# Attention heads in groups of four on TensorE, and a null product over all 128 rows

## The chip, the cores and the metric

The kernel runs on one core of one Trainium2 chip. The metric is device time in microseconds (us) of one execution. The times before are three runs; the profile is one further execution, whose own time and span are given below.

## What is computed

Eight batches of 256 rows and 128 features go through an attention layer with 16 heads of 64, then through a gated feed-forward network (FFN) with quantised weights and activations, and the result is added to the input. In short:

```
xn = ln(x) * g_norm
q = xn @ Wq (16 heads of 64);  k, v = halves of xn @ Wkv   (one k and v for all heads)
k, v = [null_kv ; k], [null_kv ; v]                        (one null key ahead of the 256)
sim = 8 * (q/|q| * q_scale) @ (k/|k| * k_scale).T + bias   (null bias, relative position bias from an MLP)
attn = softmax(causal(sim));  out = attn @ v
y = ln(out @ Wout) * g_out
x + FFN(y)      (y and the hidden layer quantised to 8 bits by their largest magnitude)
```

The causal mask is known ahead: rows 0 to 127 need 129 keys, rows 128 to 255 need 257.

## The kernel before

Five engines run programs of their own and meet at semaphores. After a prologue (bias table, projections of batch 0) comes the main part, a sequence of steps, one for each head of each batch: 16 steps for batch 0 ("first"), 96 for batches 1 to 6, 16 for batch 7 ("last") and 16 more to drain ("flush"). `over_batches` calls `step` on every engine; the order of the work is written out by hand, as lags in steps behind the scores of a head.

For a pair of heads, TensorE makes the scores with a contraction over 64 rows (L758): the two heads of a pair sit on the upper and lower 64 rows and their products run side by side, into `score_ps[0]` and `score_ps[1]`. That pair of PSUM banks is the only one, so the scores of the next pair wait for semaphore `scored`. VectorE adds the bias and finds the row maxima (L1084). ScalarE takes exponents with the row sums (L574), VectorE inverts the sums (L1090), GpSimd multiplies (L434). Five steps behind, TensorE transposes the probabilities in three 128x128 pieces (L769), ScalarE copies them to `pT` (L543), and eight steps behind TensorE multiplies them with v (L850): there the output has 64 columns for a head, and the two heads again run side by side into the two halves of `val_ps`. VectorE copies that to `oT` (L1076), TensorE multiplies by Wout (L736) into `misc`, summing over all heads of the batch. A float32 product is issued as two passes, so L758 and L850 have eight passes for a pair of heads.

The null key's share of the output is a product of its own: `null_weights` transposes the null probabilities of 16 heads (L729), ScalarE copies them to `pnT`, 16 rows, and L826 multiplies by `unull`, 16 rows, and closes the sum in `misc`.

In the same steps the next batch is prepared: x is normalised (L920) and transposed (L616), kv (L622), k (L629); q is made in four quarters (L636), squared (L487), its norm summed (L948), raised to the power -1/2 on GpSimd (L388), normalised (L954), transposed (L652) and copied to `qT` (L959). The previous batch's y gets its statistics (L1112), is normalised (L1119), transposed (L833), scaled (L1147). One PSUM bank, `qT_ps`, serves all these transposes in turn.

In the drained steps the FFN's weights are quantised on VectorE (`ffn_weights`) and turned on TensorE. Then `amax` (L1181) starts the FFN.

So on TensorE an even step is scores (64 rows), transposes and other work of full rows and columns, and an odd step is transposes, then values (64 columns).

Of the kernel before, what the change touches and what calls it, by code (L numbers as in the profile page):

```python
# [54 lines left out]
L_EXP, L_RECIP, L_NORM, L_TRANS, L_EVAC, L_VAL, L_OUT = 1, 2, 2, 5, 6, 8, 9  # L55

Q_FIRST = 4
Q_SQUARE, Q_POWER, Q_NORMALISE, Q_TRANS, Q_SPLIT = 1, 2, 3, 4, 5

FLUSH = 16  # L60


class Step:


    def __init__(self, b, parity, h, kind="loop"):
        self.b, self.parity, self.h, self.kind = b, parity, h, kind
        self.live = kind != "flush"

        self.next = (b + 1, 1 - parity) if kind in ("loop", "first") else None  # L70
        self.prev = (b - 1, 1 - parity) if kind != "first" else None

    def head(self, lag):

        h = self.h - lag
        if h >= 0:
            return (self.b * H + h, self.parity, h) if self.live else None
        return ((self.b - 1) * H + h + H, 1 - self.parity, h + H) if self.kind != "first" else None

    def quarter(self, lag):  # L80


        h = self.h - lag - Q_FIRST
        if h % 4 or not (self.next if h >= 0 else self.kind in ("loop", "last")):
            return None
        n, parity = self.next if h >= 0 else (self.b, self.parity)
        q = h % H // 4
        return 4 * n + q, q, parity

    def pair(self, lag):  # L90

        h = self.h - lag
        return self.b * HP + h // 2 if h >= 0 else (self.b - 1) * HP + (h + H) // 2
# [9 lines left out]
def over_batches(eng, step):  # L103

    for h in range(H):
        step(Step(0, 0, h, "first"))
    for b in range(1, B - 1):
        for h in range(H):
            step(Step(b, b % 2, h))
    for h in range(H):  # L110
        step(Step(B - 1, 1, h, "last"))
    for h in range(FLUSH):
        step(Step(B, 0, h, "flush"))


def build(nc, x, cond, mask, g_norm, Wq, Wkv, q_scale, k_scale, null_bias, w0, b0, g0, w1, b1, g1, w2, b2,
# [3 lines left out]
    with ExitStack() as ctx:  # L120
# [32 lines left out]
        unull = sb("unull", [H, C])  # L153
# [55 lines left out]
        pnT = sb("pnT", [H, N])  # L209
# [61 lines left out]
        null_column = sem("null_column")  # L271
# [98 lines left out]
        def _(pool):  # L370
# [44 lines left out]
            pool.memset(vnull[:, :, :], 0.0).then_inc(consts, 1)  # L415
            mlp_power(1)
# [7 lines left out]
            def step(s):  # L424
                if s.next and s.h == 8:
                    k_power(s.next[0])
                if quarter := s.quarter(Q_POWER):
                    c, q, _ = quarter
                    q_power(c, q)
                if head := s.head(L_NORM):  # L430
                    g, par, h = head
                    held(pool, inverted, g + 1, pool_passed)
# [3 lines left out]
                if s.kind == "last" and s.h == 10:  # L436
# [3 lines left out]
                if s.next and s.h == 0:  # L440
                    x_power(s.next[0])
                if s.prev and s.h == 12:
                    y_power(s.prev[0])

            over_batches(pool, step)
# [12 lines left out]
        def _(act):  # L458
# [13 lines left out]
            def v_copy(n, par):  # L472

                if not isinstance(n, int) or n > 1:
                    act.wait_ge(o_done, HP * (n - 1))
# [8 lines left out]
            def q_square(c, ps):  # L484
                act.wait_ge(q_done, c + 1)
                act.wait_ge(q_n2, c) if not isinstance(c, int) or c > 0 else None
# [37 lines left out]
            def ffn_weights(h):  # L524

                if h in (11, 12, 13):
                    k = h - 11
                    act.wait_ge(w_t, k + 1)
                    act.copy(wT[:, k, :, :], score_ps[k % 2][:, 0:IT * P].rearrange("p (t c) -> p t c", t=IT))\
                       .then_inc(w_a, 1)  # L530
                if h == 14:
# [3 lines left out]
            def step(s):  # L535
                if head := s.head(L_EVAC):
                    g, par, h = head
                    act.wait_ge(pT_done, g + 1)

                    pair = s.pair(L_EVAC)  # L540
                    if not isinstance(pair, int) or pair > 1:
                        act.wait_ge(o_done, pair - 1)
                    act.copy(pT[:, h % 4, :], trans_ps[h % 2][:, 0:3 * P]).then_inc(pT_ready, 1)  # L543
                if s.next:
                    n, par = s.next
                    if s.h == 3:
                        xT_evac(n, par, qT_ps)
                    if s.h == 7:
                        kv_evac(n, qT_ps)
                    if s.h == 11:  # L550
                        kT_evac(n, par, qT_ps)
                    if s.h == 10:
                        v_copy(n, par)
                if quarter := s.quarter(Q_SQUARE):
                    q_square(quarter[0], q_ps)
                if s.kind == "first":
                    if s.h == 11:
                        act.wait_ge(unull_done, 1)
                        act.copy(unull[:, :], misc[0:H, 0:C]).then_inc(unull_ready, 1)
                    if s.h == 15:  # L560
                        act.wait_ge(ld_misc, 16 * 5)
                        act.activation(sig[:, :], clips[:, :], ACT.Exp, scale=-1.0).then_inc(sig_exp, 1)
                if s.kind == "flush":
                    ffn_weights(s.h)
                if s.prev and s.h == 7:
                    m, _ = s.prev
                    act.wait_ge(n_done, m + 1)
                    act.copy(pnT[:, :], null_out).then_inc(n_ready, 1)
                if head := s.head(L_EXP):
                    g, par, h = head  # L570
                    for t, cols in ((1, slice(0, KEYS1)), (0, slice(KEYS1, KEYS1 + KEYS0))):

                        act.wait_ge(scored, 2 * g + (1 if t else 2))
                        act.activation(prob[:, par, h, cols], score[:, h % 4, cols], ACT.Exp, scale=-1.0,  # L574
                                       bias=negmax[:, par, h, t:t + 1],
                                       accum_out=rowsum[:, par, h, t:t + 1]).then_inc(exped, 1)

            over_batches(act, step)
# [33 lines left out]
        def _(pe):  # L612
# [33 lines left out]
            def qT_make(c):  # L646
                pe.wait_ge(q_norm, c + 1)
                if not isinstance(c, int) or c > 0:
                    pe.wait_ge(qT_ready, c)
# [614 lines left out]
```

## Time and profile before

| | us |
|---|---|
| median of three runs (lowest, highest) | 321.32 (320.86, 322.37) |
| the profiled execution | 322.74 |
| its span, first to last instruction | 320.9 |
| TensorE busy in the span | 275.6 |
| VectorE, ScalarE, GpSimd busy | 251.8, 228.5, 209.9 |
| mean granted TensorE clock | 0.961 |
| one step each on the way: subtraction for `wql` (L1102), two heads normalised on GpSimd (L434, four instructions) | 1.20, 1.66 |

Busy time counts an instruction from its start to its end. On TensorE a pass starts before the one ahead of it has ended, so the distance between starts says what a pass costs, and its duration does not. The same holds to a lesser degree on VectorE and ScalarE.

### The profile page before, as it was taken

The page shows a single profiled execution, that of the slowest core. Times are in us where ns is not written, and L with a number is a line of the kernel's source. Part 1 is how long each engine was busy: PE and PEld are TensorE (multiplying, and loading weights), DVE is VectorE, ACT ScalarE, POOL GpSimd, SP SyncE. Part 2 cuts the span into 40 slices and gives each one's busy share as a digit, 9 for nine tenths or more (in the row PEclk, how much of TensorE's full clock was granted, in tenths as well). Part 3 has the DMA queues.
Part 4 walks back from the last instruction along what each step waited for, and adds up shares of the span by engine and source line. Part 5 has one row for each costly group of instructions (what it writes and reads, how often), then busy time and mean ns, then how long its engine had stood idle before and what let it go on. Part 6 is the DMA issues. An engine that isn't in the chain of part 4 may idle for free.

```text
span 320.9 us, 7447 instructions
## 1 busy us (share of the span) xinstructions
PE 275.6 (86%) x2151; PEld 205.2 (64%) x2152; DVE 251.8 (78%) x1068; ACT 228.5 (71%) x771; POOL 209.9 (65%) x395
## 2 busy tenths in 40 slices
PE   0797899999899989998999899989998998956341
PEld 0345677787678767876777678767876776731031
DVE  3877887877887788778877887788778766848995
ACT  1454688887788778877887788778877897436761
POOL 3665797786778677767776778678867746311413
PEclk9999799999999999999999999999999999975957
DMA  4459000000000000000000000000000002000004
GB/s 140 109 129 224 1 1 3 0 2 1 3 0 3 3 1 2 0 3 1 3 0 3 0 3 3 0 0 4 3 0 2 1 3 67 2 2 0 0 2 135
DMA packets 13084, 6.90 MB, mean 21 GB/s; under 512 B 1953, under 2 KB 12913, under 8 KB 13042
## 3 DMA queue, kind: packets, MB, share of 16 engines
q1 hardware_dynamic: 12466, 6.13, 7.2%
q8 instruction: 20, 0.33, 0.4%
q10 hardware_dynamic: 576, 0.26, 0.3%
q14 instruction: 22, 0.18, 0.2%
HBM read 5.31 MB, written 1.07 MB: 20 GB/s over the span
## 4 chain that ended last, share of the span: by engine, by line
PE 56%; DVE 24%; POOL 10%; issue 5%; DMA 1%; ACT 1%; ACTq 0%; POOLq 0%; DVEq 0%
PE bank L758 12%; PE bank L850 12%; PE bank L769 10%; PE bank L736 7%; PE bank L636 4%; DVE score L1084 3%; PE bank L652 3%; POOL rq L388 3%; POOL prob L434 3%; DVE qT L959 2%; DVE qn L948 2%; DVE hmax L1171 2%; DVE oT L1213 2%; POOL ors L388 2%; DVE xn L920 2%
## 5 line engine op out<-in xcount | busy, mean ns | idle before, releaser
L434 POOL TENSOR_SCALAR prob<-prob,rrow 128x258 f32<-128x258 f32 (+1 forms) x256 | 109.9, 446 | 50.1 <-DVE rrow L1090 47.0
L574 ACT ACTIVATE prob<-score,negmax 128x258 f32<-128x258 f32 (+1 forms) x256 | 114.4, 451 | 10.5 <-DVE negmax L1084 10.5
L1084 DVE CUSTOM_DVE_ANT_0 score<-bank,bias 128x258 f32<-128x258 f32 (+1 forms) x256 | 80.5, 352 | 22.5 <-PE bank L758 21.7
L543 ACT COPY pT<-bank 128x384 f32<-128x384 f32 x128 | 61.1, 478 | 31.2 <-PE bank L850 29.1
L769 PE MATMUL bank<-ident,prob 128*128 128x128 f32 x384 | 66.7, 283 | 0.0
L758 PE MATMUL bank<-kT,qT 64*128 64x258 f32 (+1 forms) x512 | 60.1, 354 | 1.2 <-DVE negmax L1084 1.0
L388 POOL TENSOR_TENSOR rq<-qn,neghalf 128x8 f32<-128x8 f32 x32 | 54.2, 1694 | 2.7
L850 PE MATMUL bank<-pT,val 128*64 128x256 f32 (+1 forms) x512 | 55.7, 338 | 0.1
L758 PEld LDWEIGHTS bank<-kT,qT 64*128 64x128 f32 x512 | 44.7, 188 | 15.6 <-issue 11.0
L574 ACT ACTIVATION_READ_ACCUMULATOR prob<-score,negmax 128x1 f32 x256 | 48.8, 191 | 0.0
L769 PEld LDWEIGHTS bank<-ident,prob 128*128 128x128 f32 x384 | 42.5, 141 | 8.9 <-issue 0.3
L850 PEld LDWEIGHTS bank<-pT,val 128*64 128x64 f32 x512 | 31.2, 136 | 20.0 <-issue 9.9
L736 PE MATMUL bank<-wout,oT 128*128 128x128 f32 x256 | 37.9, 276 | 0.0
L1076 DVE COPY oT<-bank 128x256 f32<-128x256 f32 x64 | 26.7, 418 | 11.7 <-PE bank L850 10.3
L736 PEld LDWEIGHTS bank<-wout,oT 128*128 128x128 f32 x256 | 33.0, 192 | 0.2 <-issue 0.2
L948 DVE TENSOR_REDUCE qn<-sq 128x8 f32<-128x512 f32 x32 | 21.7, 679 | 6.5 <-ACT sq L487 6.5
L487 ACT ACTIVATE sq<-bank 128x512 f32<-128x512 f32 x32 | 19.1, 598 | 9.9 <-PE bank L636 6.2
L954 DVE TENSOR_TENSOR qn<-bank,rq 128x512 f32<-128x512 f32 x32 | 21.7, 679 | 0.6 <-POOL rq L388 0.4
L959 DVE COPY qT<-bank 128x512 f32<-128x512 f32 x32 | 21.7, 679 | 0.2 <-PE bank L652 0.2
L1084 DVE DVE_READ_ACCUMULATOR2_ANT negmax<- 128x1 f32 x256 | 21.0, 82 | 0.0
L652 PE MATMUL bank<-ident,qn 128*128 128x128 f32 x128 | 20.0, 281 | 0.9 <-DVE qn L954 0.9
L1090 DVE RECIPROCAL rrow<-rowsum 128x2 f32<-128x2 f32 x128 | 20.4, 160 | 0.2 <-ACT prob L574 0.2
(157 smaller groups left out, 344.4 us busy)
## 6 DMA issues: line engine op xcount, KB each, us to landing
bias<-relative_table SPq DMA_DIRECT2D x8, 256.0 KB, 5.2
out_dram<-prob SPq DMA_DIRECT2D x4, 256.0 KB, 2.6
X<-in_x_dram SPq DMA_DIRECT2D x1, 896.0 KB, 12.2
prob<-in_L_cond_Wq_dram SPq DMA_DIRECT2D x1, 512.0 KB, 5.8
wout<-in_L_cond_Wout_dram SPq DMA_DIRECT2D x1, 512.0 KB, 13.4
prob<-in_L_ffn_w_down_dram SPq DMA_DIRECT2D x1, 176.0 KB, 2.5
X<-in_x_dram SPq DMA_DIRECT2D x1, 128.0 KB, 4.2
prob<-in_L_ffn_w_gate_dram SPq DMA_DIRECT2D x1, 128.0 KB, 2.1
```

The costliest lines, as they stand in the source:

```text
L388: pool.tensor_tensor(dst, src, neghalf[:, 0:width], ALU.pow).then_inc(done, 1)
L434: pool.tensor_scalar(prob[:, par, h, cols], prob[:, par, h, cols], rrow[:, par, h, t:t + 1], 1.0, ALU.mult, ALU.mult).then_inc(normed, 1)
L543: act.copy(pT[:, h % 4, :], trans_ps[h % 2][:, 0:3 * P]).then_inc(pT_ready, 1)
L574: act.activation(prob[:, par, h, cols], score[:, h % 4, cols], ACT.Exp, scale=-1.0, bias=negmax[:, par, h, t:t + 1], accum_out=rowsum[:, p ...
L652: last = pe.transpose(qT_ps[:, k * P:k * P + P], head_pair, ident[:, :])
L736: pe.matmul(y_out(t), oT[:, par, k, t * P:t * P + P], wout[:, k, :], start=k + t == 0, stop=False, skip_group_check=True)
L758: product = pe.matmul(score_ps[a][:, at:at + KEYS1 - c0], qT[s.parity][rows, k, t * P:t * P + P], kT[s.parity][rows, c0:KEYS1], start=not ...
L769: last = pe.transpose(trans_ps[h % 2][:, k * P:k * P + P], prob[:, par, h, c0:c0 + P], ident[:, :])
L850: last = pe.matmul(val_ps[a * D:a * D + D, i0:N], val[par][:, blk, :], pT[:, (h - 1 + a) % 4, c0:c1], start=blk == 1, stop=blk == 0, skip_ ...
L948: dve.tensor_reduce(qn2[:, q, :], sq[:, :, :], AX.X, ALU.add).then_inc(q_n2, 1)
L959: dve.tensor_copy(qT[par][:, 4 * (q // 2):4 * (q // 2) + 4, P * (q % 2):P * (q % 2) + P], qT_ps[:, :].rearrange("p (k i) -> p k i", k=4)). ...
L1084: dve.tensor_tensor_reduce(score[:, slot, c0:c0 + w], ps[:, c0:c0 + w], bias[:, s.h, 0:w], -1.0, -3.0 * NEG, ALU.add, ALU.min, negmax[:, p ...
```

## The change

Steps of one head become groups of four. There are 34 groups, four for each of eight batches and two to drain; `Group` has the group's number `at`, the batch `b` and the place `g` (0 to 3) in it.

TensorE's order in a group is now: scores of its first pair of heads (A); values of all four heads of the group before the last one, into a whole PSUM bank; scores of its second pair (B); then everything with full rows: transposes of two heads of the last group, qT of a quarter, the next quarter's q, transposes of the other two heads, y products, and the transposes and products of x, kv, k, y. Before the last of these a wait for the qT copy of the quarter (`qT_ready`) stands in each group.

VectorE copies values to `oT` once for four heads (512 columns) and inverts row sums once for a pair (128x4). The null product's operands `pnT` and `unull` get 128 rows, of which 112 are zero, set by two memsets on GpSimd. Filler transposes behind the first scores are 10 instead of 16. In the last group the turns of the FFN's weights stand ahead of the last y products; the last batch's y is finished after the groups.

```
+        pnT = sb("pnT", [P, N])            # was [H, N]; unull likewise
+            pool.memset(unull[:, :], 0.0).then_inc(null_zero, 1)
+            pool.memset(pnT[:, :], 0.0).then_inc(null_zero, 1)
...
+            def values(at):
+                m, g = at // GB, at % GB
+                pe.wait_ge(pT_ready, GH * (at + 1))
+                if g == 0:
+                    pe.wait_ge(v_ready, m + 1)
+                if at > 0:
+                    pe.wait_ge(oT_ready, at)
+                for pair in range(2):
+                    for blk, c0, c1, i0 in ((1, 0, N, 0), (0, N, N + P, P)):
+                        for a in range(2):
+                            last = pe.matmul(val_ps[a * D:a * D + D, pair * N + i0:pair * N + N], val[m % 2][:, blk, :],
+                                             pT[:, 2 * pair + a, c0:c1], start=blk == 1, stop=blk == 0,
+                                             skip_group_check=True)
+                last.then_inc(o_done, 1)
...
+            def group(s, masked):                                   # TensorE
+                turned = s.at - 1 if 1 <= s.at <= GB * B else None
+                summed = s.at - 2 if s.at >= 2 else None
+                if s.live:
...
+                    scores(s, 0, masked)
+                if summed is not None:
+                    values(summed)
+                if s.at == 0:
+                    keep_busy(10)
+                if s.live:
+                    scores(s, 1, masked)
+                if turned is not None:
+                    turn(turned, 0)
+                    turn(turned, 1)
+                if s.quarter is not None:
...
+                    qT_make(s.quarter)
+                if s.made is not None:
...
+                    q_make(s.made, s.made % 4, s.made // 4 % 2, q_ps)
+                if turned is not None:
+                    turn(turned, 2)
+                    turn(turned, 3)
+                if s.at == GB * B + 1:
+                    for k in range(3):
+                        w_turn(k)
+                    down_scale_turn()
+                if summed is not None:
+                    y_products(summed)
+                if s.g == 1 and s.prev is not None:
+                    y_null(s.prev)
+                if s.quarter is not None:
+                    pe.wait_ge(qT_ready, s.quarter + 1)
+                if s.g == 0 and s.prev is not None:
...
+                    null_weights(s.prev)
+                if s.next is not None:
+                    if s.g == 0:
+                        xT_make(s.next, qT_ps)
+                    if s.g == 1:
+                        kv_make(s.next, qT_ps)
+                    if s.g == 2:
+                        kT_make(s.next, qT_ps)
+                if s.first and s.g == 1:
+                    null_output()
+                if s.g == 3 and s.prev is not None:
+                    yT_make(s.prev)
...
+            def group(s):                                           # VectorE
...
+                if s.live:
+                    score_pair(heads(s.at)[0:2])
+                if s.g == 0 and s.b > 1:
+                    yT_evac(s.b - 2)
+                if s.g == 2 and s.prev is not None:
+                    y_stats(s.prev)
+                if s.g == 2 and s.next is not None:
+                    k_norm2(s.next)
+                if s.g == 1 and s.next is not None:
+                    xT_split_low(s.next, s.next % 2)
+                if s.g == 0 and s.next is not None and not s.first:
+                    x_normalise(s.next)
+                if s.quarter is not None:
+                    q_normalise(s.quarter, s.quarter % 4, q_ps0[s.quarter] if s.quarter < 4 else q_ps)
+                if s.at >= 2:
+                    oT_copy(s.at - 2)
...
+                if s.live:
+                    score_pair(heads(s.at)[2:4])
+                    invert(heads(s.at)[0:2])
+                if s.g == 2 and s.prev is not None:
+                    y_normalise(s.prev)
+                if s.g == 2 and s.next is not None:
+                    k_normalise(s.next)
...
+                if s.quarter is not None:
+                    qT_evac(s.quarter, s.quarter % 4, s.quarter // 4 % 2)
+                if s.g == 3 and s.b + 2 < B:
+                    x_stats(s.b + 2)
+                if s.made is not None:
+                    q_norm2(s.made, s.made % 4)
+                if s.live:
+                    invert(heads(s.at)[2:4])
```

ScalarE's order in a group: exponents of heads 0 and 1, pT copies of the last group's heads 0 and 1, exponents of head 2, the square of a quarter of q, pT copy 2, exponents of head 3, pT copy 3, then the copies for x, kv, v, k. GpSimd's: the power for a quarter of q, normalisation of the last group's second pair, the powers for y and k (g = 2), normalisation of this group's first pair, the power for x (g = 3).

## Rows read from the trace of the kernel before

**Rows 1.** The page, part 1: busy time, share of the span and instructions

```profile
PE 275.6 (86%) x2151; PEld 205.2 (64%) x2152; DVE 251.8 (78%) x1068; ACT 228.5 (71%) x771; POOL 209.9 (65%) x395
```

**Rows 2.** Windows by batch: stretch, its length, busy time by engine, granted clock

```profile
26.38:55.44 29.06, 26.45 (x202) 20.49 (x202) 23.33 (x109) 20.66 (x80) 21.27 (x38) 0.94 0.17 40
55.44:87.23 31.79, 30.37 (x255) 23.67 (x253) 25.33 (x120) 25.26 (x90) 23.78 (x46) 1.00 0.01 2
...
214.38:246.17 31.79, 30.37 (x254) 23.68 (x253) 25.93 (x122) 25.27 (x90) 23.96 (x47) 1.00 0.01 2
246.17:287.84 41.67, 37.55 (x319) 28.72 (x317) 28.81 (x132) 29.10 (x99) 19.87 (x47) 0.97 0.06 15
```

**Rows 3.** Timeline of TensorE around one pair of heads: start, us, merged instructions

```profile
150.00 0.87 PE L850 MATMUL bank<-pT,val 128*64 128x256 f32 x8
150.80 0.93 PE L758 MATMUL bank<-kT,qT 64*128 64x258 f32 x8
151.66 0.55 PE L769 MATMUL bank<-ident,prob 128*128 128x128 f32 x3
...
152.75 0.60 PE L652 MATMUL bank<-ident,qn 128*128 128x128 f32 x4
153.18 0.61 PE L736 MATMUL bank<-wout,oT 128*128 128x128 f32 x4
153.63 0.49 PE L769 MATMUL bank<-ident,prob 128*128 128x128 f32 x3
```

**Rows 4.** The same in narrow windows: later passes of the same two blocks

```profile
150.49 0.39 PE L850 MATMUL bank<-pT,val 128*64 128x128 f32 x4
...
151.34 0.39 PE L758 MATMUL bank<-kT,qT 64*128 64x129 f32 x4
```

**Rows 5.** Timeline of TensorE around the null product

```profile
140.00 0.61 PE L736 MATMUL bank<-wout,oT 128*128 128x128 f32 x4
140.54 0.71 PE L826 MATMUL bank<-unull,pnT 16*128 16x128 f32 x4
141.18 0.55 PE L769 MATMUL bank<-ident,prob 128*128 128x128 f32 x3
```

**Rows 6.** Timeline of TensorE: its two idle stretches in a batch, with the releaser

```profile
116.63 0.44 PE L833 MATMUL bank<-ident,yn 128*128 128x128 f32 x2 [0.96 <-DVE qT L959]
...
124.93 0.44 PE L616 MATMUL bank<-ident,xn 128*128 128x128 f32 x2 [0.46 <-DVE qT L959]
```

**Rows 7.** Timeline: the other engines' starts within a batch

```profile
130.92 0.93 PE L758 MATMUL bank<-kT,qT 64*128 64x258 f32 x8
...
132.03 0.43 DVE L1084 CUSTOM_DVE_ANT_0 score<-bank,bias 128x258 f32<-128x258 f32 x1 [0.57 <-PE bank L758]
...
132.67 0.41 DVE L1084 CUSTOM_DVE_ANT_0 score<-bank,bias 128x258 f32<-128x258 f32 x1
...
155.02 0.48 ACT L543 COPY pT<-bank 128x384 f32<-128x384 f32 x1 [0.60 <-PE bank L850]
155.40 0.67 DVE L948 TENSOR_REDUCE qn<-sq 128x8 f32<-128x512 f32 x1
155.40 0.51 ACT L574 ACTIVATE prob<-score,negmax 128x258 f32<-128x258 f32 x1
...
155.99 0.68 DVE L959 COPY qT<-bank 128x512 f32<-128x512 f32 x1
...
156.29 0.48 ACT L543 COPY pT<-bank 128x384 f32<-128x384 f32 x1
...
156.59 1.67 POOL L388 TENSOR_TENSOR rq<-qn,neghalf 128x8 f32<-128x8 f32 x1
```

**Rows 8.** Timeline of TensorE at the last null product

```profile
282.36 0.71 PE L826 MATMUL bank<-unull,pnT 16*128 16x128 f32 x4
```

**Rows 9.** Window of one block of scores in batch 0, columns as in rows 2

```profile
33.37:34.96 1.59, 1.59 (x9) 1.18 (x8) 1.42 (x2) 1.48 (x7) 1.43 (x1) 0.50 0.00 0
```

More of the change, by code:

```diff
@@ L52, with __init__, heads @@
 TABW = N + P - 1
[L55 to L93, printed above, removed]
+GB = 4
+GH = H // GB
+class Group:
+    def __init__(self, at):
+        self.at = at
+        self.b, self.g = at // GB, at % GB
+        self.par = self.b % 2
+        self.live = self.b < B
+        self.first = self.b == 0
+        self.next = self.b + 1 if self.b + 1 < B else None
+        self.prev = self.b - 1 if self.b > 0 else None
+        c = GB * self.b + self.g + 2
+        self.quarter = c if c < GB * B else None
+        self.made = c + 1 if 4 <= c + 1 < GB * B else None
+def heads(at):
+    b, h = at // GB, at % GB * GH
+    return [(b * H + h + i, b % 2, h + i) for i in range(GH)]
 def held(eng, sem, value, passed):
@@ L100, in held, with over_groups @@
     eng.sem_inc(passed, 1)
[L103 to L113, printed above, removed]
+def over_groups(group):
+    for at in range(GB * B + 2):
+        group(Group(at))
 def build(nc, x, cond, mask, g_norm, Wq, Wkv, q_scale, k_scale, null_bias, w0, b0, g0, w1, b1, g1, w2, b2,
@@ L422, in _, with normalise @@
                 q_power(q, q)
[L424 to L432, printed above, removed]
+            def normalise(pair):
+                held(pool, inverted, pair[0][0] // 2 + 1, pool_passed)
+                for _, par, h in pair:
                     for t, cols in ((1, slice(0, KEYS1)), (0, slice(KEYS1, KEYS1 + KEYS0))):
@@ L439, in step @@
                     pool.memset(wrow[:, 2, IT - 1, IL:P], 0.0).then_inc(w_pad, 1)
[L440 to L445, printed above, removed]
+            over_groups(group)
+            y_power(B - 1)
             for k in range(4):
@@ L522, in _, with exponent @@
             act.copy(wqh[:, :], wq[:, :]).then_inc(wq_high, 1)
[L524 to L531, printed above, removed]
+            def exponent(head):
+                g, par, h = head
+                for t, cols in ((1, slice(0, KEYS1)), (0, slice(KEYS1, KEYS1 + KEYS0))):
+                    act.wait_ge(scored, 2 * g + (1 if t else 2))
+                    act.activation(prob[:, par, h, cols], score[:, h % 4, cols], ACT.Exp, scale=-1.0,
+                                   bias=negmax[:, par, h, t:t + 1],
+                                   accum_out=rowsum[:, par, h, t:t + 1]).then_inc(exped, 1)
@@ L532, in ffn_weights @@
                     act.wait_ge(w_t, 4)
                     act.copy(sdrow[:, :], score_ps[1][:, 0:C]).then_inc(w_a, 1)
[L535 to L576, printed above, removed]
@@ new lines, in scores @@
+            def scores(s, pair, masked):
+                g, par, h = heads(s.at)[2 * pair]
+                if g > 0:
+                    pe.wait_ge(scored, 2 * g)
+                if masked:
+                    for a in range(2):
+                        pe.matmul(score_ps[a][:, 0:KEYS1 + KEYS0], ones_row[:, :], mrow[:, s.b, 0:KEYS1 + KEYS0],
+                                  start=True, stop=True)
+                for t, at, c0 in ((1, 0, 0), (0, KEYS1, P + 1)):
+                    for a in range(2):
+                        rows = slice(a * D, a * D + D)
+                        product = pe.matmul(score_ps[a][:, at:at + KEYS1 - c0],
+                                            qT[par][rows, h // 2, t * P:t * P + P], kT[par][rows, c0:KEYS1],
+                                            start=not masked, stop=True, skip_group_check=True)
+                        if t == 0:
+                            product.then_inc(s_done, 1)
@@ new lines, in group @@
+                if s.made is not None:
+                    if s.made % 4 == 0:
+                        if s.first:
+                            pe.wait_ge(wq_low, 1)
+                        pe.wait_ge(xT_low, s.next)
+                    q_make(s.made, s.made % 4, s.made // 4 % 2, q_ps)
+                if turned is not None:
+                    turn(turned, 2)
+                    turn(turned, 3)
+                if s.at == GB * B + 1:
+                    for k in range(3):
+                        w_turn(k)
+                    down_scale_turn()
@@ L1155, in scales @@
+            over_groups(group)
+            y_stats(B - 1)
+            y_normalise(B - 1)
+            yT_evac(B - 1)
             def scales(k):
```

413 lines of the change are left out of this document (188 added, 225 removed).

## Prediction, made before the changed kernel ran

> **What bounds the kernel now.** I read the page first: TensorE 86% busy, VectorE 78, ScalarE 71, GpSimd 65 [rows 1]. Four engines this full cannot be ranked by shares of a whole run, so next came the table by stage, cut at the first score product of each batch [rows 2]. Batches 1 to 6 take 31.79 us each, to the hundredth, with TensorE busy 30.4, VectorE 25.9, ScalarE 25.3 and GpSimd 24.0. TensorE hardly stops there, at a granted clock of 1.00, its 2.4 GHz level. Then I read the timeline of TensorE alone, since a busy TensorE need not be a working one [rows 3 to 6].
>
> Inside a block of one shape its passes start at even distances: four passes of 128 columns take 0.43 to 0.45, so 0.109 each, and a pass of 256 columns costs twice that, 0.216 [rows 3, 4]. Between shapes the distance grows. A block of values, eight passes in four side-by-side pairs, needs 2 x 0.216 + 2 x 0.109 = 0.65 and takes 0.80: 0.05 is lost before its third pair (0.49 from its start instead of 0.43), 0.10 before the next block. A block of scores takes 0.86 where 0.65 would do: 0.11 lost at its start (0.54 to its third pair), 0.10 at its end. The full-row block behind it loses 0.06 at its start (three transposes take 0.55, where those that follow a full-row product take 0.49) and 0.10 at its end (140.00 to 140.54 for four passes that need 0.44) [rows 3 to 5]. One pair of heads has three changes of shape and loses 0.15 + 0.21 + 0.16 = 0.52; eight pairs are 4.2 a batch. The null product on 16 rows adds two more: 0.64 for four passes that need 0.44, 0.10 lost ahead of it and 0.06 behind, 0.36 a batch [rows 5].
>
> The rest are real waits: the transposes of yn and of xn stand idle for 0.96 and 0.46 until VectorE has copied qT [rows 6]. With the weight loads that such a wait uncovers they make up the remainder. The books of a batch: 31.79 = 25.4 of streaming + 4.2 + 0.36 + 1.86 of waits.
>
> **The change, part by part.**
>
> *Shapes.* In four heads the order was scores, full rows, values, full rows and so on, six changes. Now it is scores A, values of two pairs, scores B, full rows: four changes, 2 x 0.21 + 0.15 + 0.16 = 0.73 instead of 1.04, so 0.31 x 4 = 1.26 saved a batch. Scores followed directly by values is a neighbourhood that the trace does not show. I take the 0.10 with which every block ends and the 0.05 with which values start, since in the three neighbourhoods seen each end costs the same. Bounds: nothing at all, 0.15 x 4 = 0.6 more saved; as dear as the entry of scores, 0.05 x 4 = 0.2 lost. The Trainium skill (TensorEngine Tiling (Array Packing), Key Properties) says that changing the tiling mode, not just the tile, drains TensorE; it gives no price, and the gaps above agree with it.
>
> *Null product over 128 rows.* The same four passes without a change of shape: 0.36 saved a batch, 2.9 in eight. It can't be less than 0: the y products ahead of it write the same tile at 0.11 a pass. The Trainium skill (TensorEngine Tiling (Array Packing), When to Use Tiling) advises four-fold row tiling for a contraction of up to 32, which speaks against this edit: by it the 16 rows would be the cheap form. The row shows no two of the four passes side by side, and the 0.64 against 0.44, so the measurement decides. The two memsets for it are on GpSimd before batch 0 and end before the first normalisation needs it.
>
> Without any wait a batch would take 25.4 + 2.9 + 0.3 (a small gap before scores B, below) = 28.6.
>
> *VectorE.* Eight oT copies of 256 columns become four of 512, 0.60 apart as L948 and L959 are; sixteen reciprocals become eight. Its 25.9 falls to about 24.5. ScalarE and GpSimd keep their work. The FFN weights' memsets and DMAs move to g = 1 of the last batch, some 15 us before VectorE reads them.
>
> *Waits, by walking one group on four engines.* Distances between starts: scores of a head on VectorE 0.56 (0.64 with an inversion), 512 columns 0.60, exponents of a head 0.89, pT copy 0.38 [rows 7], square 0.50, GpSimd 0.84 a head; a q power is 0.33 + 1.67 and begins 0.2 behind its input. VectorE starts on scores 1.11 after their block began (130.92, 132.03) [rows 7]. Time 0 is TensorE's start on scores A.
>
> g = 3, the plain group. VectorE works on A from 1.11 to 2.23. TensorE ends values at 2.31, but B may start only when both heads of A are released, 2.37: 0.06 lost in every group. B reaches VectorE at 3.48; until then it does q normalise and oT, to 3.44. TensorE: two turns to 3.94, qT 4.38, q 5.08, turns 5.73, y 6.60, yT, next group 6.93. ScalarE: exponents 1.62 to 3.42, two pT copies to 4.58, exponent 5.48, square, pT, exponent, pT to 7.65; values of the next group want that pT at 7.8. The last pair is inverted at 7.6, 0.44 before the next scores reach VectorE. GpSimd: the next group's q power ends 2.0 to 2.4 into it, where VectorE wants it at 2.24.
>
> g = 0: VectorE first evacuates yT (0.85) and normalises x (0.62), so qn is late and qT starts at 4.44, not 3.94: with null and x transposes 7.65. g = 1: y null and kv, four passes each: 7.65. g = 2: y statistics and k norm (1.24) put q normalise at 3.5, so qT is late by 0.3, scores B end at 5.8, and y normalise and k scaling (1.25) still stand ahead of the qT copy, which ends at 7.8. The new wait on qT_ready closes every full block; behind it stand the turn of k and the next group's scores. TensorE is ready for it at 7.0 and waits 0.96: 8.2. Sum 30.4, with the 0.06 of each group 30.7. So the old waits (1.86) go and new ones (0.5 + 1.3 + 0.3) come, and the gain is 1.1 a batch, 6.6 in six.
>
> *Ends.* Nothing changes before the first score (26.38). Batch 0 was 29.06 [rows 2]. In its group 0 VectorE sets the pace: scores A, q normalise, x statistics, scores B, x normalise, wql (1.20), qT copy, 7.8 in all, where two pairs took 7.0 before (26.38 to 33.37). Group 1 gets null_output (1.85) and null_values: 8.1. Then 7.0 and 6.9: 29.8, a loss of 0.8. In such a thin stretch the clock can fall: it was granted at 0.50, the 1.2 GHz level, when the block of scores at 33.37 took 1.59, not 0.86 [rows 9]; 0 to 1.5 more in the range for that. Fewer filler transposes (10 for 16) lie under VectorE's work on A. The last batch to amax took 41.67 [rows 2]. Now: groups of 6.9, 6.4, 6.0 and 6.2, then the turns of group 31 behind GpSimd's normalisation, y of group 30 and values of 31, to 5.5 after the last scores' group; the weight turns, once in idle steps, stand ahead of the last y products and wait for VectorE's two last weight steps (2.1), so these start at 9.0 and the null product ends at 10.3; amax follows the start of the null product by 5.5 as before (282.36, 287.84) [rows 2, 8]. 25.5 + 9.9 + 5.5 = 40.9, 0.8 gained. The FFN's 33.06 (287.84 to 320.9) stays.
>
> Sum: 26.38 + 29.8 + 6 x 30.7 + 40.9 + 33.06 = 314.3, against the 320.9 of the profiled span, 6.5 less. That execution took 322.74, of which 1.9 lie outside the span, and is 1.4 above the median; 321.32 - 6.5 = 314.8, and I say 314.5.
>
> **Rivals.**
> *Waits vanish* (0.2). The late qT copy and the late qn meet slack, as the engines' own sums (24 to 25.3) leave 3 us even in 28.6. Against it: VectorE's fixed order, walked above. A period of 28.6 to 29.6 gives 321.3 - 6 x 2.7 = 305.
> *Waits eat all* (0.15). Steps of four heads are coarse. If releases come some 0.3 later in each group than I walked, the period is 31.8 and the ends decide: 319 to 322.
> *Slower* (0.12). One ring: scores B wait for VectorE to finish A, A waits behind the inversion of the last pair, that for ScalarE's last exponent, and all full-row work stands behind B. Its slack is 0.44. If a head costs ScalarE the sum of its durations (0.51 + 0.19 + 0.39 + 0.19 = 1.28) and not 0.89, it is 1.5 later, a group takes 7.9 to 8.3 and the period is 33: 321.3 + 7 + 1 = 329. It decides from 0.7 later in each group on. For it speaks ScalarE's 6.0 of work in 6.93; against it, that 0.89 holds wherever two of its instructions meet [rows 7].
> *Not what it says* (0.03). If the gaps belong to the semaphore waits at block starts and not to shapes, they stay, and only the new waits come: 324.
>
> The forecast has 0.5: period 30.2 to 31.2, 311 to 318.
>
> **The numbers.** 314.5 us. The range of 304 to 322 takes in the first two rivals and leaves out the last two and a little below: 0.8. What can be told from no change is half a per cent, 1.6 us: faster 0.75 (forecast, first rival, a third of the second), same 0.10, slower 0.15.
>
> **In the profile after.** Shapes: blocks of 16 value passes at 1.45, scores still 0.86, no gap around the null product, 0.44 for it. Waits: a period of 30.7; g = 2 the longest group, with an idle TensorE ahead of the k turn put down to the qT copy, and shorter ones ahead of the qT turns of g = 0 and 2 put down to qn. Ends: batch 0 near 30. I am wrong if gaps of the same total stand between half the blocks, if TensorE waits on negmax for more than 0.1 a group, or if its idle passes 3 us a batch.

## The result, and the profile after

The changed kernel takes 319.25 us, median of four runs (318.27 to 319.96), against 321.85 of the kernel before in the same comparison: a ratio of 0.989 with a 95% interval of 0.985 to 0.993. A second comparison, listed below, gave 0.990 (0.987 to 0.994). The interval leaves no change out, so it is faster, by about 1%. The ratio and its interval are those on record for the whole comparison; the two medians by themselves give 0.992. The forecast, 314.5 from 321.32, was 0.979: by the ratio about half of that gain came, by the medians 2.6 of 6.8 us. The profiled execution took 319.06, its span 317.3.

The page of the changed kernel, part 1, answers to [rows 1]:

```profile
PE 265.6 (84%) x2145; PEld 207.5 (65%) x2146; DVE 241.7 (76%) x972; ACT 226.2 (71%) x771; POOL 209.5 (66%) x397
```

TensorE is busy 10 us less and the span is only 3.6 shorter. The windows by batch say where the rest is; cut as in [rows 2], at the first scores of a batch and at amax, columns the same:

```profile
25.38:58.44 33.06, 27.48 (x207) 22.41 (x208) 22.91 (x104) 21.88 (x82) 19.73 (x38) 0.85 0.17 41
58.44:88.26 29.82, 29.25 (x254) 23.88 (x253) 23.79 (x108) 25.12 (x94) 24.17 (x47) 1.00 0.01 2
...
118.64:149.02 30.38, 29.33 (x253) 23.84 (x252) 24.81 (x110) 24.86 (x91) 23.84 (x47) 1.00 0.01 2
...
240.17:284.22 44.05, 35.95 (x307) 28.18 (x306) 27.66 (x117) 27.65 (x96) 20.80 (x47) 0.92 0.06 14
```

| stage | before | forecast | after |
|---|---|---|---|
| to the first scores | 26.38 | 26.38 | 25.38 |
| batch 0 | 29.06 | 29.8 | 33.06 |
| batches 1 to 6 | 190.7 | 184.2 | 181.7 |
| last batch, to amax | 41.67 | 40.9 | 44.05 |
| FFN | 33.06 | 33.06 | 33.08 |

The six middle batches gain 9.0, more than forecast; both ends lose, 4.0 and 2.4, where a loss of 0.8 and a gain of 0.8 were forecast. Both ends also show a lower granted clock, 0.85 and 0.92, than the 0.94 and 0.97 of [rows 2]. (The first scores come between 25.4 and 27.3 in the kernels below; nothing was changed ahead of them, and I count that as scatter.)

Now the middle. The timeline of TensorE in batch 3, groups g = 0 and 1:

```profile
121.87 0.87 PE L805 MATMUL bank<-ident,prob 128*128 128x128 f32 x6
123.30 0.63 PE L657 MATMUL bank<-ident,qn 128*128 128x128 f32 x4 [0.56 <-issue]
...
127.39 1.52 PE L793 MATMUL bank<-pT,val 128*64 128x256 f32 x16
128.90 0.93 PE L776 MATMUL bank<-kT,qT 64*128 64x258 f32 x8
129.76 0.88 PE L805 MATMUL bank<-ident,prob 128*128 128x128 f32 x6
...
132.27 1.06 PE L746 MATMUL bank<-wout,oT 128*128 128x128 f32 x8
133.16 0.61 PE L753 MATMUL bank<-unull,pnT 128*128 128x128 f32 x4
133.61 0.61 PE L627 MATMUL bank<-wkv,xTr 128*128 128x128 f32 x4
```

Sixteen value passes take 1.51 from start to next start, which is the 1.45 of the forecast plus the 0.06 until B may start; scores still take 0.86 (128.90 to 129.76). The null product takes 0.45 (133.16 to 133.61), like any four passes. The 0.06 is a real wait: B starts at 128.90, 2.37 behind A as walked, right after VectorE has released A (128.84). Where B is released earlier, as in the last batch, the same block takes 1.45:

```profile
248.05 1.52 PE L793 MATMUL bank<-pT,val 128*64 128x256 f32 x16
249.50 0.93 PE L776 MATMUL bank<-kT,qT 64*128 64x258 f32 x8
```

The four groups of batch 3 start 7.89, 7.62, 7.95 and 6.92 apart; the walk, with its 0.06, had 7.71, 7.71, 8.26 and 6.99.

The two waits that were forecast are there. The first is 0.56 ahead of the qT turns of g = 0 (row two). The profile names no releaser for it, only "issue", but VectorE's qn of this quarter ends just before, at 123.20:

```profile
122.52 0.68 DVE L974 TENSOR_TENSOR qn<-bank,rq 128x512 f32<-128x512 f32 x1
```

The second is in g = 2. There, TensorE and below it VectorE in the same stretch:

```profile
138.24 0.63 PE L657 MATMUL bank<-ident,qn 128*128 128x128 f32 x4
...
139.39 0.82 PE L805 MATMUL bank<-ident,prob 128*128 128x128 f32 x6
140.70 1.13 PE L746 MATMUL bank<-wout,oT 128*128 128x128 f32 x8 [0.49 <-DVE yn L1127]
141.73 0.44 PE L634 MATMUL bank<-ident,kz 128*128 128x128 f32 x2
```

```profile
137.45 0.69 DVE L974 TENSOR_TENSOR qn<-bank,rq 128x512 f32<-128x512 f32 x1
...
139.85 0.70 DVE L1127 TENSOR_SCALAR yn<-bank,omv,ors 128x128 f32<-128x128 f32 x2
140.47 0.61 DVE L957 SCALAR_TENSOR_TENSOR kz<-kv,rk,qks 128x128 f32<-128x128 f32 x2
140.99 0.69 DVE L979 COPY qT<-bank 128x512 f32<-128x512 f32 x1
```

The place is as walked; the size is a little less (the group takes 7.95, not 8.26), and the name is another. The y products of a new batch may not write their bank before yn of the last batch has been read from it, and that wait comes first. It is about 0.66, from the end of six transposes of 0.109 behind 139.39 to 140.70. When the y products end, the qT copy is all but done and costs 0.15.

The start. TensorE in groups 0 and 1 of batch 0, then the windows of these two groups:

```profile
28.90 0.66 PE L657 MATMUL bank<-ident,qn 128*128 128x128 f32 x4
33.22 0.69 PE L621 MATMUL bank<-ident,xn 128*128 128x128 f32 x2 [3.67 <-DVE qT L979]
33.84 1.67 PE L776 MATMUL bank<-kT,qT 64*128 64x258 f32 x8
36.93 1.66 PE L776 MATMUL bank<-kT,qT 64*128 64x258 f32 x8 [1.42 <-DVE negmax L1104]
```

```profile
25.38:33.84 8.46, 4.30 (x32) 3.21 (x32) 6.42 (x27) 3.73 (x16) 5.25 (x8) 0.85 0.63 155
33.84:44.82 10.98, 9.56 (x57) 7.92 (x56) 5.21 (x24) 7.14 (x25) 4.22 (x10) 0.65 0.01 1
```

TensorE stands idle for 3.67 behind its few products, and the granted clock falls to half in that stretch (0.54 on average from 31.00 to 33.80). It is 0.50 from 33.84 to 41.40 and 0.99 from there to 44.80, so the first 7.6 of group 1 run at half: scores in 1.6 instead of 0.86, the group in 10.98 instead of the 8.1 forecast.

The end. TensorE in the last batch and behind it, then two pieces of the chain that ended last:

```profile
259.39 1.13 PE L746 MATMUL bank<-wout,oT 128*128 128x128 f32 x8 [0.32 <-DVE yn L1127]
...
264.88 0.90 PE L805 MATMUL bank<-ident,prob 128*128 128x128 f32 x6 [0.33 <-ACT pT L531]
...
267.67 1.52 PE L793 MATMUL bank<-pT,val 128*64 128x256 f32 x16 [0.78 <-ACT pT L531]
```

```profile
276.31 0.34 PE bank L710 x3
276.65 0.34 PE bank L718 x2
277.00 1.59 PE bank L746 x8
278.59 0.87 PE bank L753 x4
```

With no qT and q work between them, the third and fourth head's transposes wait for ScalarE to empty the two banks, and the values that follow wait for its last pT copy. The y products at 277.00 stand behind the weight turns. The clock fell here too: it was granted at 0.54 from 276.83 to 279.28 and at 0.50 from there to amax, and the eight passes of y take 1.59, where they take 0.89 in the middle (132.27 to 133.16). (The timeline has these y products at 276.83 and the null product at 278.38, a little earlier than the chain; the sums below go by the timeline, as the forecast did.)

### The profile page after: what moved, and what is told of

Its sections match the earlier page's. It is cut to its first block, busy times and chain, and to the rows that moved or that the text cites. A ratio compares the mean times of both kernels' runs of the same rounds, so it can differ in the third digit from the quotient of the medians.

```text
span 317.3 us, 7259 instructions
## 1 busy us (share of the span) xinstructions
PE 265.6 (84%) x2145; PEld 207.5 (65%) x2146; DVE 241.7 (76%) x972; ACT 226.2 (71%) x771; POOL 209.5 (66%) x397
## 4 chain that ended last, share of the span: by engine, by line
PE 62%; DVE 19%; issue 5%; ACT 2%; POOL 0%; DVEq 0%; POOLq 0%; ACTq 0%
PE bank L776 15%; PE bank L805 11%; PE bank L793 11%; PE bank L746 9%; DVE score L1104 5%; PE bank L641 5%; PE bank L657 4%; DVE hmax L1212 2%; DVE oT L1254 2%; DVE yn L1127 2%; DVE oT L1095 2%; DVE prob L1239 1%; PE bank L753 1%; DVE ost L1118 1%; PE bank L627 1%
## 5 line engine op out<-in xcount | busy, mean ns | idle before, releaser
L412 POOL TENSOR_SCALAR prob<-prob,rrow 128x258 f32<-128x258 f32 (+1 forms) x256 | 108.6, 442 | 44.2 <-DVE rrow L1112 41.5
L1104 DVE CUSTOM_DVE_ANT_0 score<-bank,bias 128x258 f32<-128x258 f32 (+1 forms) x256 | 76.6, 354 | 29.3 <-PE bank L776 26.5
L531 ACT COPY pT<-bank 128x384 f32<-128x384 f32 x128 | 57.8, 477 | 15.2 <-PE bank L805 15.2
L805 PE MATMUL bank<-ident,prob 128*128 128x128 f32 x384 | 55.1, 280 | 1.0 <-ACT pT L531 1.0
L805 PEld LDWEIGHTS bank<-ident,prob 128*128 128x128 f32 x384 | 43.5, 142 | 9.8 <-issue 1.9
L793 PE MATMUL bank<-pT,val 128*64 128x256 f32 (+1 forms) x512 | 48.7, 332 | 0.9 <-ACT pT L531 0.8
L746 PE MATMUL bank<-wout,oT 128*128 128x128 f32 x256 | 35.0, 281 | 3.3 <-DVE yn L1127 3.3
L746 PEld LDWEIGHTS bank<-wout,oT 128*128 128x128 f32 x256 | 31.7, 195 | 4.7 <-issue 4.7
L1112 DVE RECIPROCAL rrow<-rowsum 128x4 f32<-128x4 f32 x64 | 11.2, 175 | 16.1 <-ACT prob L521 16.1
L1095 DVE COPY oT<-bank 128x512 f32<-128x512 f32 x32 | 21.8, 681 | 1.9 <-PE bank L793 1.8
```

Of the source, the lines that this page charges most:

```text
L746: pe.matmul(y_out(t), oT[:, m % 2, k, t * P:t * P + P], wout[:, k, :], start=k + t == 0, stop=False, skip_group_check=True)
L793: last = pe.matmul(val_ps[a * D:a * D + D, pair * N + i0:pair * N + N], val[m % 2][:, blk, :], pT[:, 2 * pair + a, c0:c1], start=blk == 1, ...
L805: last = pe.transpose(trans_ps[h % 2][:, k * P:k * P + P], prob[:, par, h, c0:c0 + P], ident[:, :])
L1095: dve.tensor_copy(oT[:, m % 2, 2 * g:2 * g + 2, :].rearrange("p k n -> p (k n)"), val_ps[:, :])\
L1104: dve.tensor_tensor_reduce(score[:, h % 4, c0:c0 + w], ps[:, c0:c0 + w], bias[:, h, 0:w], -1.0, -3.0 * NEG, ALU.add, ALU.min, negmax[:, pa ...
```

## The experiments

Each expectation is quoted as it stood before its run. The period is the distance between the first scores of neighbouring batches in the middle. Periods and stage lengths are differences of starts in the run's own trace; times without an interval are one execution each. Beside them the kernel before took 322.81 (sections 1, first run, to 4), 322.44 (5 to 8) and 322.94 (9, 10 and the timed run of 1). Whole times of single executions differ for other reasons too, by 0.2 to 1.9 us in the start of the first scores alone, so the readings go by stages.

**1. The null product alone, on the kernel before.**

```
-        unull = sb("unull", [H, C])
+        unull = sb("unull", [P, C])
...
-        pnT = sb("pnT", [H, N])
+        pnT = sb("pnT", [P, N])
...
+            pool.memset(unull[:, :], 0.0).then_inc(null_zero, 1)
+            pool.memset(pnT[:, :], 0.0).then_inc(null_zero, 1)
...
-                    act.copy(pnT[:, :], null_out).then_inc(n_ready, 1)
+                    act.copy(pnT[0:H, :], null_out).then_inc(n_ready, 1)
```

> The kernel before, with only the null product changed: pnT and unull have 128 rows. Theory (a change of shape on TensorE costs 0.15 to 0.2, whatever the operands do): the block L826 shrinks from 0.64 to 0.44, the gaps ahead of it and behind it go, the period of batches 1 to 6 falls from 31.79 to 31.43 (0.36 less), the run by 2 to 3 us. Rival (the gaps belong to the semaphore waits at block starts): the product still waits on n_ready and the period stays 31.79.

320.57 against 322.81. The period is 31.42 to 31.45 in every batch. Its TensorE around the product:

```profile
138.69 0.61 PE L739 MATMUL bank<-wout,oT 128*128 128x128 f32 x4
139.13 0.61 PE L829 MATMUL bank<-unull,pnT 128*128 128x128 f32 x4
139.58 0.49 PE L772 MATMUL bank<-ident,prob 128*128 128x128 f32 x3
```

0.44, 0.45, and a following block that starts with no gap, where [rows 5] had 0.54, 0.64 and a gap on either side; L829 has the same semaphore wait as before. The 0.36 is the shape's; how much of it is the change of shape and how much the form on 16 rows, this run does not part.

Timed in five rounds:

> The kernel before with the null product over 128 rows, timed: 8 x 0.36 = 2.9 us less, 0.991 of before.

0.992 (0.989 to 0.995), 320.15 against 322.94. So this part alone gives about as much as the whole change does.

**2. The null product back on 16 rows, in the changed kernel.**

```
-                    pe.matmul(y_out(t), pnT[:, ...], unull[:, :], ...
+                    pe.matmul(y_out(t), pnT[0:H, ...], unull[0:H, :], ...
```

> The changed kernel, with the null product back on 16 rows. Theory (shape): the period of batches 2 to 6 rises from 30.4 by 0.36 to 30.75, as group g = 1 has no wait that could take it up (7.62 to about 7.98). Rival (semaphores): 30.4.

323.21, with its first scores 1.9 later than in the changed kernel. The period is 30.77 (122.22 to 152.99), 0.38 more; g = 1 takes 7.99 instead of 7.61.

**3 and 4. One added pass, between shapes and within one.**

```
                 for pair in range(2):                                  # run 3, in values()
+                    if pair:
+                        pe.transpose(trans_ps[0][:, 3 * P:4 * P], ident[:, :], ident[:, :])
...
+                if i == 0:                                             # run 4, in turn()
+                    pe.transpose(trans_ps[0][:, 3 * P:4 * P], ident[:, :], ident[:, :])
```

> The changed kernel plus one full-row transpose of the identity between the two pairs of value products in every group: no semaphore, one pass, two more changes of shape. Theory (shape): the pass costs its 0.11 and the changes 0.25 to 0.31 more, scores B start 0.36 to 0.42 later; the period rises by 4 x 0.4 less what the waits in g = 0 and g = 2 (0.65 and 1.03) take up, so by 0.8 to 1.6. Rival (semaphores): it costs 0.11 a group like the same pass inside full-row work.

> Control for the run before it: the same extra transpose of the identity, but as the first pass of the full-row transposes of a group, so no change of shape is added. Both theories: 0.11 a group where TensorE does not wait later in the group (g = 1 and 3), taken up by the waits in g = 0 and 2: the period rises by 0.2 to 0.44.

Run 3 took 327.26 and run 4 321.99. Run 3, TensorE in g = 1, from the values to scores B and past them; run 4 in the same place:

```profile
129.69 0.87 PE L795 MATMUL bank<-pT,val 128*64 128x256 f32 x8
130.50 0.33 PE L792 MATMUL bank<-ident 128*128 128x128 f32 x1
130.76 0.87 PE L795 MATMUL bank<-pT,val 128*64 128x256 f32 x8
131.56 0.93 PE L776 MATMUL bank<-kT,qT 64*128 64x258 f32 x8
```

```profile
129.18 1.52 PE L793 MATMUL bank<-pT,val 128*64 128x256 f32 x16
130.69 0.93 PE L776 MATMUL bank<-kT,qT 64*128 64x258 f32 x8
```

From the first value pass to scores B it is 1.87 against 1.51, so 0.36 later. That is a lower bound for what the pass and its two changes cost, since in the 1.51 B was held for 0.06 and in run 3 it is not: VectorE has released A at 131.16, 0.40 before B starts. Against the 1.45 of the block that is not held, it is 0.42: 0.11 for the pass and 0.31 for the two changes, with no semaphore near them. In groups without other waits the length follows: g = 1 and g = 3 grow by 0.36 and 0.35 in run 3, by 0.11 and 0.12 in run 4. The period grows by 0.6 (31.00) and 0.12 (30.52), less than the 0.8 to 1.6 and the 0.2 to 0.44 expected, since g = 0 and g = 2 took up all of it: they wait on VectorE anyway, and g = 0 is even 0.08 shorter in both. The semaphore rival is out.

**5. The clock in batch 0.**

```
                     qT_make(s.quarter)
+                if s.at == 0:
+                    keep_busy(30)
```

> The changed kernel plus 30 filler transposes in group 0 of batch 0, behind the qT transposes, where TensorE is idle for 3.67 until VectorE has copied qT. Theory A (batch 0 is long, 33.06, mostly because that idle stretch let the clock fall to 0.50 for the 10 us in which group 1 runs): the granted clock stays 1.00 longer, group 1 falls from 10.98 to 8 or so, batch 0 to 30 to 31, the run by 2 to 3 us. Rival B (group 1 is long because of VectorE's order, and TensorE's clock only follows): group 1 stays above 10 whatever the clock.

317.31. Batch 0 takes 30.11 instead of 33.06 (33.43 in the second trace of the changed kernel, run 10). TensorE, and the windows of the two groups:

```profile
29.71 3.44 PE L671 MATMUL bank<-ident 128*128 128x128 f32 x30
```

```profile
25.71:33.91 8.20, 7.33 (x62) 6.39 (x63) 6.42 (x27) 3.74 (x16) 5.00 (x8) 1.00 0.64 150
33.91:42.20 8.29, 6.86 (x56) 5.61 (x56) 5.22 (x24) 6.93 (x25) 4.48 (x10) 1.00 0.00 0
```

Work that is of no use, in a stretch where TensorE has nothing to do, makes the next group 2.7 shorter. VectorE's busy time is the same in both (6.42, then 5.21 and 5.22), so it is not VectorE's order that made group 1 long. The Trainium skill (TensorE: Matmul & The Clock Gate, HAM oscillation) says that idle gaps between bursts of matmuls bring the half rate back; the trace agrees, at 2.95 us here. In this run the last batch still takes 44.02, with the last y products at a granted clock of 0.50: the filler holds the clock in batch 0 only.

**6. wql behind the qT copy.** The order of two VectorE instructions in group 0 of batch 0.

> The changed kernel with the 1.20 us subtraction for wql moved behind the qT copy in group 0 of batch 0. Theory: TensorE's idle stretch in group 0 shrinks from 3.67 to 2.5 and group 0 from 8.46 to 7.3. If the clock rule of batch 0 is idleness alone, the stretch at clock 0.50 shrinks or goes too and batch 0 gains 1.2 plus up to 2.5; if any idle stretch of this size is enough, batch 0 gains only the 1.2.

318.07. TensorE's idle stretch is 2.50, group 0 takes 7.03 instead of 8.46, group 1 still 10.63 at a mean clock of 0.68. The clock is lost later than in the changed kernel: group 0 and the first scores of group 1 (0.93) run at full rate, and the fall comes in the second idle stretch, 1.43 ahead of scores B. In run 5, with fillers in the first stretch, the same 1.43 did not bring it. Batch 0 gains 1.8, the first 1.4 by the order itself.

**7. The order at the end.**

```
                 if summed is not None:
                     y_products(summed)
                 if s.g == 1 and s.prev is not None:
                     y_null(s.prev)
+                if s.at == GB * B + 1:            # was ahead of y_products, and yT_make after it
+                    w_turn(0) ; w_turn(1) ; yT_make(B - 1) ; w_turn(2) ; down_scale_turn()
...
+                    y_stats(B - 1) ; ffn_weights(3) ; y_normalise(B - 1) ; ffn_weights(4)   # VectorE
```

> The changed kernel with the last y products and null product ahead of the turns of the FFN's weights, y statistics and normalisation between VectorE's two last weight steps. Theory: the last y products wait only for the oT copy, not for the weights; y_null ends 2.5 to 3 earlier and amax falls from 284.22 to 281.2 to 281.7, the run by 2.5 to 3 us. Rival: the weights are late in any order (VectorE does them all anyway) and the FFN start moves by under 1 us.

316.07. From the last batch's first scores to amax it is 41.15 instead of 44.05. TensorE:

```profile
274.39 1.16 PE L746 MATMUL bank<-wout,oT 128*128 128x128 f32 x8 [0.79 <-DVE oT L1096]
275.38 0.61 PE L753 MATMUL bank<-unull,pnT 128*128 128x128 f32 x4
275.83 0.33 PE L710 MATMUL bank<-identb,wintb 128*128 128x128 bf16 x3
```

The last y products now wait for the oT copy alone and start 34.42 behind the batch's first scores, not 36.66. They and the null product run at full rate (0.99 and 0.45). So the 2.9 is not the order's alone. The other runs with the old order at the end part it: in three of them the clock was still 1.00 at the last y products, and the last batch took 43.08 (run 2), 43.10 (run 4) and 42.95 (run 8); with the clock fallen it took 44.05 and 44.02 (run 5). About 1.0 of the 2.9 is the clock, and about 1.9 is the order. Whether the new order keeps the clock up, or had it by chance, no run decides; run 10 has it up as well.

**8. VectorE's order in the middle.**

```
+                if s.g == 0 and s.b > 1:  yT_evac(s.b - 2)
+                if s.g == 2 and s.prev is not None:  y_stats(s.prev)
+                if s.g == 2 and s.next is not None:  k_norm2(s.next)
                 if s.live:
                     score_pair(heads(s.at)[0:2])          # these three stood behind it
...                                                        # and x_normalise goes behind score_pair [2:4]
```

> The changed kernel with VectorE's order changed: yT copy (g = 0), y statistics and k norm (g = 2) ahead of scores A, where VectorE stands idle for 0.8 to 1.1, and x normalise behind scores B. Theory (what is left of waits on TensorE is VectorE's queue, qn late in g = 0, yn and then qT late in g = 2): g = 0 falls from 7.90 to about 7.25, g = 2 from 7.95 to about 7.0, the period from 30.4 to 28.8, the run by 9 to 10 us. Rival (the four engines are so full that a wait removed in one place comes back in another, ScalarE's above all): the period stays above 30.

311.83. The period is 29.1 from batch 1 on, not the 28.8 expected; g = 0 takes 7.34, g = 2 7.21 (expected 7.25 and 7.0). TensorE's value and score blocks in g = 0:

```profile
118.44 1.52 PE L793 MATMUL bank<-pT,val 128*64 128x256 f32 x16
120.14 0.93 PE L776 MATMUL bank<-kT,qT 64*128 64x258 f32 x8 [0.18 <-DVE negmax L1104]
```

Most of both waits is gone. What is left in g = 0 is that scores B now start 0.18 later, since the yT copy runs a little into scores A.

**9. More work on ScalarE.**

```
+                if s.live and s.at >= 4:
+                    act.copy(dose[:, :], wqh[:, 0:512].bitcast(F32))
                 if s.live:
                     exponent(heads(s.at)[3])
```

> The changed kernel with one more copy of 512 columns (about 0.6 us) on ScalarE ahead of the last exponents of every group from batch 1 on; its result is not used. Theory (TensorE and VectorE's order set the group, the ring through ScalarE has a slack of 0.4 to 0.5): g = 3 grows by 0.1 to 0.2, the others by about as much or less, the period by 0.2 to 0.7. Rival (the slower one of the prediction: the ring through ScalarE's last exponent sets every group): the period grows by 4 x 0.6 = 2.4.

One execution at 323.75. The added copy and the exponent behind it:

```profile
119.50 0.64 ACT L555 COPY dose<-wqh 128x512 f32<-128x512 f32 x1
120.02 0.53 ACT L522 ACTIVATE prob<-score,negmax 128x258 f32<-128x258 f32 x1
```

and TensorE's values in g = 1:

```profile
129.32 1.52 PE L796 MATMUL bank<-pT,val 128*64 128x256 f32 x16 [0.37 <-ACT pT L532]
```

0.52 in each group, 2.1 in a batch, and the period is 30.76, 0.37 more, all of it in g = 1 (7.99 for 7.61); g = 3, where I had expected it, takes 6.94. The ring through ScalarE's last exponent does not set the groups in the middle. But ScalarE is not far behind: with 0.52 more, its last pT copy holds up the values by 0.37 in g = 1, and in g = 0, where the wait for qn takes it up. So in g = 1 ScalarE's slack is only about 0.14.

**10. All mends at once** (5, with 20 fillers, 6, 7 and 8), and the changed kernel beside it on the same chip. Ratios are to the kernel before, 322.94 there.

> The changed kernel with the four mends at once: VectorE's order, the tail's order, wql behind the qT copy, 20 filler transposes in group 0. Theory (the terms are independent, each in a stage of its own): batch 0 about 29, period 29.1, last batch to amax about 41.2, first score at 25.7; span 25.7 + 29 + 6 x 29.1 + 41.2 + 33.1 = 303.6, run 305.5, 0.950 of before. Rival (they share their gain): over 308.

> The changed kernel again, as it is, beside the mended one on the same chip: 0.989 of before, 319.2. Its span again without the clock's fall would be 3 us less.

The mended kernel: 306.61 (306.03 to 308.16), ratio to before 0.952 (0.948 to 0.956). The changed kernel again: 319.56 (318.84 to 321.55), 0.990 (0.987 to 0.994), with batch 0 at 33.43. The mended kernel's windows:

```profile
26.26:55.25 28.99, 26.75 (x227) 22.20 (x227) 23.19 (x104) 21.69 (x82) 19.93 (x37) 1.00 0.19 44
...
113.44:142.54 29.10, 28.84 (x253) 23.86 (x253) 24.78 (x110) 24.58 (x91) 24.17 (x47) 1.00 0.01 2
...
229.97:271.21 41.24, 35.37 (x307) 27.53 (x306) 27.62 (x118) 25.93 (x94) 21.06 (x46) 0.97 0.05 14
```

The period and the last batch come out at 29.1 and 41.2, as in runs 8 and 7. Batch 0 takes 29.0, with its group 0 as in run 6 (7.05) and its group 1 as in run 5 (8.29). So the terms add; the whole came out 1.1 us above the 305.5 expected.

## Why the prediction was right in the middle and wrong in size

**Shapes: right.** The neighbourhood that the trace before did not show, scores followed by values, costs what was taken for it: 16 value passes and their ends take 1.45 (plus 0.06 of wait where B is held), and run 3 measures 0.31 for two changes, as the sum had it for two fewer. The null product: 0.36 forecast, 0.36 and 0.38 measured in either kernel. The row decided rightly against the rule on small contractions. (In the working, 0.31 x 4 is 1.24 and not 1.26; nothing hangs on it.)

**Waits in the middle: right in place and nearly in size, one with the wrong name.** The period is 30.32 to 30.43 for 30.7 (29.82 in batch 1, where no yT copy stands in g = 0 yet), and each group is within 0.31 of the walk. I overlooked the wait of the first y products on yn. The sum hardly changed, since yn and the qT copy stand in one VectorE queue; the mend does, for by this reading a qT copy moved ahead of yn would not free the y products (not tried). Run 8 confirms the cause for both: it is VectorE's order.

**Batch 0: the first mis-sized term, the clock.** The step "29.8, a loss of 0.8 [...] 0 to 1.5 more in the range for that" put the clock outside the sum. The walk itself was good: with the clock held, batch 0 takes 30.11 (run 5). The fall costs 2.95, twice the most that the range allowed for. I had the idle stretch in my own walk, VectorE busy to 7.8 while TensorE had 4 us of work, and in [rows 9] a block that such a stretch had slowed; there only one block of scores and its neighbours ran slow, and I took that as the size, where a whole group followed.

**Last batch: the second.** "25.5 + 9.9 + 5.5 = 40.9" measured 27.5 + 10.7 + 5.8 = 44.05. Of the 3.1 too much, 2.0 are the four groups. The groups of the last batch were made shorter by taking TensorE's missing work out of the plain group (6.0 and 6.2). The trace shows 6.7 and 7.2: by its rows, without qT and q between them the transposes wait for ScalarE to empty the two banks, y for yn, and the first values that no scores cover for ScalarE's last pT copy. That reading was not tried in a run. The other 1.1 is the clock again, put at nothing in this sum: the y products start 9.16 behind the last scores' group, for 9.0 forecast, but then run at half. In runs 2, 4 and 8, where the clock was up there, the two last terms add up to 15.3 to 15.4, as forecast. The weight turns ahead of y were forecast as a delay, rightly; run 7 shows that an order without it was to be had, 1.9 cheaper. Even so the mended tail, 41.2, is hardly better than the 41.67 before.

**Books.** From a forecast span of 314.3 to the 317.3 measured: -1.0 ahead of the first scores, +3.3 batch 0, -2.5 middle, +3.1 last batch. Of the 6.4 too much at the ends, about 4 are the clock. That the total still landed well inside the range is owed to the middle, which came out 2.5 better than the sum had it; that was not foreseen.

**Rivals.** *Waits vanish* did not come by itself, but it was the right bound: with another order of VectorE the period is 29.1, where it gave 28.6 to 29.6. *Waits eat all* names the right time, 319 to 322, for the wrong reason: it put the loss in the middle, where the period is 30.4 and not 31.8; it was the ends that took 6.4 of the 9.0 gained there. *Slower* through ScalarE's ring is refuted by run 9: 0.37 a batch, not 2.4. *Not what it says* is refuted by runs 1 to 4.

## What to carry to other kernels

When a change makes the steady part of a pipeline denser, walk its first and last rounds as carefully as a middle one, with every engine in the walk: they hold fewer covers, and here they gave back 6.4 of 9.0 us. An idle stretch of TensorE has a price apart from its own length: here 2.95 us in the work that followed at half clock, while 30 fillers in the stretch cost nothing (group 0 took 8.20 with them, 8.46 without). Look for it at the end as well, where about 1 us went the same way. And for a matmul on few rows amid full-width ones, whose passes do not run side by side with others, try padding with zeros: here it gave 2.8 us for two memsets.

## What was not expected of the hardware

The half clock outlasted the idle stretch by far. In the changed kernel it set in within the 3.67 us idle and stayed at 0.50 to 41.40, 8.2 us after the stretch had ended, although TensorE was busy all the time from 38.00 on. In the kernel before, 1.55 idle were followed by about 3.4 at 0.50 (32.90 to 36.10 at 0.50, 1.00 from 36.80). And with almost the same instructions at the end, the clock at the last y products was 1.00 in some executions and 0.50 in others, which moves the last batch by about 1.0 us (runs 2 and 4 against 5).
